# Step sizes of a Mamba block: x products ahead of the dt products, du turned in two halves around them, and ScalarE's copies in that order

## The chip, the cores and the metric

The kernel runs on one core of one Trainium2 chip. The metric is the device time of one execution in microseconds, the median of several executions. Five engines run their own instruction streams and meet only at semaphores: TensorE (PE), VectorE (DVE), ScalarE (ACT), GpSimd (POOL) and SyncE (SP, which here issues the DMAs). Each takes its instructions in the order in which they stand, so a wait holds everything behind it on that engine.

## What is computed

The reference is a two-layer network on x of 4 batches x 512 tokens x 256 features. The change touches one stage of the first layer, the step sizes of a Mamba block. Cut to what matters:

```python
u2 = silu(conv(u) + conv_b)                    # 4 x 512 tokens x 512 channels
dbl = u2 @ W_x                                 # 48 columns: dt_low (16), Bm (16), Cm (16)
dt = softplus(dt_low @ W_dt + b_dt)
A = -exp(A_log)
def step(h, inp):                              # the scan that follows
    dA = exp(dt_t[:, :, None] * A)
    h = dA * h + (dt_t * u_t)[:, :, None] * B_t[:, None, :]
    y = einsum('bdn,bn->bd', h, C_t)
```

softplus(v) is computed as max(v, 0) + ln(1 + exp(-|v|)), with a correction for what 1 + e loses in rounding.

## The kernel before

Channels lie on partitions: a batch is 4 chunks (m) of 128 channels x 512 tokens. The stage walks over the batches in the order `ORDER = (2, 3, 0, 1)`; i counts the places in that order, 0 to 3, and h or r is a half (two chunks of channels, or two tiles of tokens). All orders are written out by hand. For each i:

- TensorE. `x_products(i, bank)` (line 911) is 4 products of u2 with W_x into PSUM bank 4 (in the profile, x8 with 512 columns each). Its two waits are on u2 and on ScalarE's copy of the x product before it, since all but the first share bank 4. `dt_products(i, h)` (line 929) is 2 products into banks 2h and 2h + 1 (x4 in the profile); it waits until VectorE has finished the half of the batch before that used these banks. The B columns are transposed into bank 5 (lines 968 to 976). `turn_du(i, banks)` (line 937) transposes du of a batch in two halves of 8 transposes. Through banks (6, 6) the second half waits for ScalarE's copy of the first; this is done for batch i - 1 after `dt_products(i, 1)`.
- ScalarE. For each half, Abs from PSUM, Exp, Ln (lines 1741 to 1745), which wait for the dt products and for VectorE to have read the last `soft_e` and `soft_l` of that half. Between the halves it copies the next x product (`dbl_out`, line 1671) and the B columns out of PSUM. After the second half `turned_du(i - 1)` (line 1702) copies the two turned halves to `duT`.
- VectorE. For each half four instructions (lines 2095 to 2102), the last of which reads PSUM and writes dt; after both halves du = u2 * dt (line 2106). There is one buffer du, so it waits until TensorE has turned both halves of du of the batch before (`s_duT_mm`, line 2105).
- SyncE. For each i it writes the C rows to DRAM, and for i = 1, 2 it spills u2, dt and duT of batch i - 1 (3 MB) once both turned halves are copied (`s_duT` at 2i). VectorE clears `decay` (line 2111) only when the C rows and both spills have landed. After them come a load of weights and the C rows for the scan.

Ahead of the stage, ScalarE's loop (lines 1688 to 1698) applies silu to the gates z (`gate_z`) and to the convolved u (`silu_out`); the last pass does `gate_z(3, 1)` and then `silu_out` of the last half. A table load follows. Behind the stage, TensorE waits for all of dt, does `d_term(0)` (line 949: zeroing and 32 small matmuls of u2 with a diagonal), turns the last du through banks (6, 4), waits for ScalarE's copies, and feeds the scan. The scan is 64 steps (4 batches x 16 states) of two halves, on all of TensorE, ScalarE, VectorE and GpSimd; the other three stages of the network follow it.

Of the kernel before, what the change touches and what calls it, by code (L numbers as in the profile page):

```python
# [19 lines left out]
ACT = mybir.ActivationFunctionType  # L20
AX = mybir.AxisListType.X

P = 128
B, S, D = 4, 512, 256
# [3 lines left out]
TILES = S // P  # L28
DI, NS, RANK, TAPS = 512, 16, 16, 4
M = DI // P  # L30
# [19 lines left out]
ORDER = (2, 3, 0, 1)  # L50
# [49 lines left out]
def program(nc, t_in, out):  # L100
    ctx = ExitStack()
    with ctx:
# [6 lines left out]
        ps = ctx.enter_context(nc.psum_tensor("ps", [P, 8, 512], F32))  # L109
# [12 lines left out]
        ident, ones, mean = w["ident"], w["ones"], w["mean"]  # L122
# [104 lines left out]
        one = sb("one", [P, 2])  # L227
        at = 0
# [3 lines left out]
        duT = [carve(b * BATCH + 2 * M * S, TILES, DI)[0] for b in range(B)]  # L232
        up, conv_end = carve(3 * BATCH + M * S, M, S + TAPS - 1)
        uc, conv_end = carve(conv_end, M, S)
        at = conv_end + 4
        soft_e, _ = carve(at, 2, 2, S)
        soft_l, soft_end = carve(at + M * S, 2, 2, S)
        lo_xc, at = carve(at, C, S)
        lo_sq, at = carve(at, C, S)
        lo_rstd, at = carve(at, S)  # L240
        s2_xc, at = carve(at, C, S)
        s2_sq, at = carve(at, C, S)
        s2_rstd, at = carve(at, S)
        dbl, dbl_end = carve(at, N)
        xn, at = carve(ARENA - B * C * S, B, C, S)
        assert soft_end <= dbl_end - N and dbl_end <= ARENA - B * C * S
        soft_r, at = carve(ARENA - B * C * S, 2, 2, S)
        du, at = carve(at, M, S)
        bt = view(w["k_aff"], [[TILES * NS, B], [NS, TILES], [1, NS]])
        at = 2 * BATCH  # L250
        decay, at = carve(at, 3, 2, S)
        dub, at = carve(at, 2, TILES, DI)
        c_rows, at = carve(at, 2, G, S)
        state, at = carve(at, SLOTS, M, S)
# [5 lines left out]
        ln_xc, at = carve(head_at + 2 * M * S, C, S)  # L260
        ln_sq, at = carve(at, C, S)
        ln_rstd, at = carve(at, S)
# [30 lines left out]
        s_dbl = sem("dbl_ready")  # L293
        s_bc = sem("bc_written")
        s_dt_mm = sem("dt_products")
        s_soft = sem("softplus_parts")
        s_dt = sem("dt_ready")
        s_z_mm = sem("z_products")
        s_sz = sem("gate_ready")
        s_z_out = sem("gates_spilled")  # L300
        s_bt_mm = sem("b_columns_turned")
        s_bt = sem("b_columns_ready")
        s_du = sem("du_ready")
        s_duT_mm = sem("du_turned")
        s_duT = sem("duT_ready")
# [27 lines left out]
        at = 0  # L333
        cw, at = carve(at, COND_W)
# [8 lines left out]
        pw_w, at = carve(at, PARTS * 2 * D)  # L343
# [453 lines left out]
        def _(pe):  # L797
# [113 lines left out]
            def x_products(i, bank):  # L911
                b = ORDER[i]
                pe.wait_ge(s_u2, (b + 2) * M)
                pe.wait_ge(s_dbl, i + 1)
                for m in range(M):
                    last = pe.matmul(ps[0:48, bank, :], w_x[:, m, :], u2[b][:, m, :],
                                     start=(m == 0), stop=(m == M - 1))
                last.then_inc(s_x_mm, 1)
# [15 lines left out]
                                     start=True, stop=True)  # L934
                last.then_inc(s_dt_mm, 1)

            def turn_du(i, banks):
                pe.wait_ge(s_du, i + 1)
                for r in range(2):
                    if i or r:  # L940
                        pe.wait_ge(s_duT, 2 * i + (r if banks[0] == banks[1] else 0))
                    for t in (2 * r, 2 * r + 1):
                        for m in range(M):
                            last = pe.transpose(ps[:, banks[r] + t % 2, m * P:(m + 1) * P], du[:, m, t * P:(t + 1) * P],
                                                ident)
                    last.then_inc(s_duT_mm, 1)

            nought = one[:, 1:2].bitcast(BF16)[:, 0:1]

# [10 lines left out]

            pe.wait_ge(s_mam, 32)
            pe.wait_ge(s_up, (B + 1) * M)
            for i, b in enumerate(ORDER):
                pe.wait_ge(s_dbl, i + 2)
                dt_products(i, 0)
                if 0 < i < B - 1:
                    x_products(i + 1, 4)
                if i:
                    pe.wait_ge(s_bt, i)
                else:  # L970
                    pe.wait_ge(s_sz, 2 * B)
                for t in range(TILES):
                    last = pe.transpose(ps[:, 5, t * 64:(t + 1) * 64], dbl[0:64, b * S + t * P:b * S + (t + 1) * P],
                                        ident[0:64, 0:64])
                last.then_inc(s_bt_mm, 1)
                dt_products(i, 1)
                if i == 0:
                    x_products(1, 4)
                else:
                    turn_du(i - 1, (6, 6))  # L980
            pe.wait_ge(s_dt, 2 * B)
            d_term(0, range(TILES))
            pe.wait_ge(s_dbl, B + 1)
            pe.wait_ge(s_bt, B)
            turn_du(B - 1, (6, 4))
            pe.wait_ge(s_duT, 2 * B)
            pe.wait_ge(s_ends, 1)

# [566 lines left out]
        def _(act):  # L1555
# [104 lines left out]
            def silu_out(b, chunks):  # L1660
                for m in chunks:
                    act.wait_ge(s_cv, b * M + m + 1)
                    act.activation(u2[b][:, m, :], uc[:, m, :], ACT.Silu,
                                   bias=wm["conv_b"][:, m:m + 1]).then_inc(s_u2, 1)

            def gate_z(i, h):
                act.wait_ge(s_z_mm, 2 * i + h + 1)
                act.activation(z_stage[ORDER[i]][:, 2 * h:2 * h + 2, :], ps[:, 4 + 2 * h:6 + 2 * h, :],
                               ACT.Silu).then_inc(s_sz, 1)

            def dbl_out(i, bank):
                act.wait_ge(s_x_mm, i + 1)
                act.activation(dbl[0:48, tok(ORDER[i])], ps[0:48, bank, :], ACT.Copy).then_inc(s_dbl, 1)
# [14 lines left out]
            for b in range(B):  # L1688
                if ORDER[b] == 0:
                    act.wait_ge(s_xh0, 1)  # L1690
                for h in range(2):
                    gate_z(b, h)
                    silu_out(b, halves[h])
                    if b == B - 1 and h == 0:
                        act.wait_ge(s_rows, 1)
                        dbl_out(0, 0)
                    if b + 1 < B:
                        tap_in(b + 1, halves[h])

            act.preload_act_table_set("natural_log_exp_and_others")  # L1700
            def turned_du(i, banks):
                if ORDER[i] == 0:
                    act.wait_ge(s_z_out, 32)
                for r in range(2):
                    act.wait_ge(s_duT_mm, 2 * i + r + 1)
                    act.activation(duT[ORDER[i]][:, 2 * r:2 * r + 2, :], ps[:, banks[r]:banks[r] + 2, :],
                                   ACT.Copy).then_inc(s_duT, 1)

            def times_b(k):
                b, n = divmod(k, NS)  # L1710
# [22 lines left out]
                act.wait_ge(s_g_turned, b + 1)  # L1733
                act.activation(view(zT[b], [[S, 2], [1, S]]), ps[:, 0:2, :], ACT.Copy).then_inc(s_g01, 1)

            for i, b in enumerate(ORDER):
                for h in range(2):
                    act.wait_ge(s_dt_mm, 2 * i + h + 1)
                    if i:
                        act.wait_ge(s_dt, 2 * i - 1 + h)  # L1740
                    act.activation(soft_e[:, h], ps[:, 2 * h:2 * h + 2, :], ACT.Abs)
                    act.drain()
                    act.activation(soft_e[:, h], soft_e[:, h], ACT.Exp, scale=-1.0)
                    act.drain()
                    act.activation(soft_l[:, h], soft_e[:, h], ACT.Ln, bias=one[:, 0:1]).then_inc(s_soft, 1)
                    if h == 0:
                        if i < B - 1:
                            dbl_out(i + 1, 4)
                        act.wait_ge(s_bt_mm, i + 1)
                        act.activation(bt[:, b], view(ps[:, 5, :], [[64, TILES], [1, NS]], RANK), ACT.Copy).then_inc(s_bt, 1)  # L1750
                if i:
                    turned_du(i - 1, (6, 6))
            act.wait_ge(s_ends, 1)
            act.drain()
            times_b(0)
            turned_du(B - 1, (6, 4))
            act.wait_ge(s_dt, 2 * B)

            for k in range(B * NS):
# [974 lines left out]
```

## Time and profile before

| | us |
|---|---|
| median of 3 runs | 1590.73 (1586.46 to 1591.49) |
| profiled execution, own time | 1589.1 |
| its span, first to last instruction | 1587.3 |
| outside the span | 1.8 |
| TensorE matmul busy | 1444.7 (91%) |
| VectorE busy | 1069.1 (67%) |
| ScalarE busy | 854.5 (54%) |
| mean granted TensorE clock | 0.957 of 2.4 GHz |

Busy shares are means over many stages, so the stage of the change has to be read by itself: it lies at about 253 to 323 us of the span. In the timelines a row is one instruction, or a run of the same instructions; "x4" is their number, and a bracket gives the idle time of the engine just before and who ended it. Times are microseconds from the start of the span.

### The profile page before, as it was taken

The numbers are of one execution on the slowest core, as the hardware profiler recorded it, in microseconds if no ns is written. First come the engines' busy times: TensorE is split into PE (matmuls) and PEld (weight loads), VectorE is DVE, ScalarE is ACT, GpSimd is POOL, SyncE is SP. The second block draws the span as 40 slices with busy tenths as digits, with TensorE's granted clock in tenths as the row PEclk, the third lists the DMA queues.
The fourth block names the chain that finished last, engine by engine and source line by source line (L and its number), as shares of the span: only waits on it lengthen the run. The fifth ranks groups of instructions, "written<-read, shape, count | busy, mean of one in ns | idle before, by whom it ended". The sixth has DMA issues, their size and how long they took to land.

```text
span 1587.3 us, 20216 instructions
## 1 busy us (share of the span) xinstructions
PE 1444.7 (91%) x7408; PEld 985.7 (62%) x7420; DVE 1069.1 (67%) x1219; ACT 854.5 (54%) x1509; POOL 477.4 (30%) x140
## 2 busy tenths in 40 slices
PE   5898798689898999998999899999989999999997
PEld 3576343488797979753443333333358888888886
DVE  6996495789899898864443557777564565565645
ACT  3433455599899898631342267777732433333332
POOL 0999020079788888400321420000000000000000
PEclk7899999799999999978999989999999999999999
DMA  7110010502232211402112122443000000000000
GB/s 269 24 61 1 1 53 2 200 31 91 97 104 107 68 66 41 163 1 41 42 38 72 59 80 61 119 132 123 1 0 0 1 14 1 0 14 1 14 1 14
DMA packets 36624, 87.61 MB, mean 55 GB/s; under 512 B 8350, under 2 KB 24948, under 8 KB 32948
## 3 DMA queue, kind: packets, MB, share of 16 engines
q1 hardware_dynamic: 36532, 86.39, 16.3%
q8 instruction: 57, 0.93, 0.2%
q14 instruction: 35, 0.29, 0.1%
HBM read 68.10 MB, written 18.21 MB: 54 GB/s over the span
## 4 chain that ended last, share of the span: by engine, by line
PE 55%; DVE 2%; ACT 2%; issue 2%; DVEq 1%; ACTq 0%
PE ps L1440 12%; PE ps L1449 12%; PE ps L1308 4%; PE ps L1381 4%; PE ps L1175 3%; PE ps L1296 3%; PE ps L1201 2%; PE ps L1137 2%; PE ps L1008 1%; ACT arena L1909 1%; PE ps L584 1%; PE ps L1350 1%; PE ps L1059 1%; PE ps L1209 1%; PE ps L1187 1%
## 5 line engine op out<-in xcount | busy, mean ns | idle before, releaser
L2593 POOL TENSOR_TENSOR arena<-arena 128x2048 f32<-128x2048 f32 x63 | 287.4, 4591 | 158.4 <-DVE arena L2133 158.3
L2133 DVE TENSOR_TENSOR_SCAN arena<-arena,ps 128x1024 f32<-128x1024 f32 x128 | 284.6, 2272 | 40.2 <-issue 20.7
L1728 ACT ACTIVATE arena<-arena,mam 128x511 f32<-128x511 f32 x256 | 165.8, 710 | 32.0 <-DVE arena L2133 32.0
L1909 ACT ACTIVATE arena<-ps,rho 128x512 f32<-128x512 f32 x256 | 159.1, 689 | 31.4 <-PE ps L1381 30.0
L2365 DVE TENSOR_REDUCE mxs<-ps 128x1 f32<-128x512 f32 x224 | 141.2, 684 | 45.2 <-PE ps L1296 43.3
L996 PE MATMUL ps<-early,arena 128*128 128x128 f32 x768 | 130.1, 278 | 20.3 <-DVE arena L2133 15.0
L1440 PE MATMUL ps<-early,arena 128*128 128x256 f32 x512 | 127.1, 380 | 2.9 <-DVE mam L2532 1.9
L1938 ACT ACTIVATE arena<-arena 128x256 f32<-128x256 f32 x192 | 85.5, 500 | 81.5 <-DVE arena L2536 50.7
L2573 POOL TENSOR_TENSOR arena<-arena 128x4096 f32<-128x4096 f32 x16 | 115.0, 7191 | 43.5 <-DVE arena L2051 43.5
L1716 ACT ACTIVATE arena<-arena,early 128x512 f32<-128x512 f32 x192 | 123.9, 709 | 4.4 <-DVE arena L2111 4.4
L1449 PE MATMUL ps<-arena 128*128 128x256 f32 x512 | 121.0, 379 | 1.2 <-issue 1.2
L1008 PE MATMUL ps<-early,arena 128*128 128x128 f32 x1024 | 121.1, 272 | 0.9 <-POOL arena L2593 0.7
L1008 PEld LDWEIGHTS ps<-early,arena 128*128 128x128 f32 x1024 | 113.8, 140 | 1.2 <-POOL arena L2593 0.8
L996 PEld LDWEIGHTS ps<-early,arena 128*128 128x128 f32 x768 | 90.3, 142 | 35.9 <-DVE arena L2133 21.9
L1440 PEld LDWEIGHTS ps<-early,arena 128*128 128x128 f32 x512 | 96.3, 190 | 19.1 <-DVE mam L2532 3.1
L1449 PEld LDWEIGHTS ps<-arena 128*128 128x128 f32 x512 | 97.2, 190 | 14.8 <-issue 1.5
L1938 ACT ACTIVATE arena<-ps,arena 128x256 f32<-128x256 f32 x64 | 26.9, 471 | 142.6 <-PE ps L1440 142.6
L1381 PE MATMUL ps<-arena 97*128 97x512 bf16 x256 | 97.0, 389 | 6.0 <-ACT arena L1909 4.4
L997 PE MATMUL ps<-arena 128*128 128x128 f32 x512 | 99.4, 276 | 0.0
L1440 PE MATMUL ps<-arena 128*128 128x256 f32 x384 | 98.8, 380 | 0.0
L2532 DVE TENSOR_TENSOR mam<-mam,ps 128x512 f32<-128x512 f32 x32 | 22.0, 687 | 97.0 <-PE ps L1440 97.0
L1296 PE MATMUL ps<-arena 96*128 96x512 bf16 x224 | 86.6, 387 | 0.0
(352 smaller groups left out, 2482.1 us busy)
## 6 DMA issues: line engine op xcount, KB each, us to landing
arena<-bc_scratch SPq DMA_DIRECT2D x32, 512.0 KB, 3.7
arena<-in_ffn SPq DMA_DIRECT2D x8, 1024.0 KB, 5.1
batch_scratch<-arena SPq DMA_DIRECT2D x2, 3072.0 KB, 8.8
arena<-batch_scratch SPq DMA_DIRECT2D x6, 1024.0 KB, 6.9
arena<-q_scratch SPq DMA_DIRECT2D x96, 64.0 KB, 2.2
arena<-k_scratch SPq DMA_DIRECT2D x96, 64.0 KB, 2.2
arena<-in_dec_w SPq DMA_DIRECT2D x1, 3855.0 KB, 16.2
arena<-in_cond SPq DMA_DIRECT2D x1, 3739.5 KB, 11.6
```

The source lines that it names most:

```text
L996: pe.transpose(ps[:, FEED + m, t * P:(t + 1) * P], dub[:, k % 2, t, m * P:(m + 1) * P], ident)
L1008: last = pe.matmul(ps[:, t, m * P:(m + 1) * P], state[:, k % SLOTS, m, t * P:(t + 1) * P], ident, start=False, stop=(k % NS == NS - 1 and ...
L1296: pe.matmul(ps[:, (hg + s) % 3, :], q[0:STACK, i, qc * P:(qc + 1) * P], k[0:STACK, i, :], start=True, stop=True).then_inc(s_s_mm, 1)
L1381: pe.matmul(ps[:, 3 + (hg + n) % 3, :], k[0:STACK + 1, i, kc * P:(kc + 1) * P], q[0:STACK + 1, i, :], start=True, stop=True).then_inc(s_t_ ...
L1440: done = pe.matmul(ps[:, bank, i * S // 2:(i + 1) * S // 2], weights[:, f, :], x, start=first and i == 0, stop=last and i == 1, skip_group ...
L1449: done = pe.matmul(ps[:, bank, half * S // 2:(half + 1) * S // 2], weights[:, f, :], x[:, i, :], start=(r == 0 and half == 0 and i == 0), ...
L1716: act.activation(dub[:, k % 2, t, :], duT[b % 2][:, t, :], ACT.Copy, scale=bt[:, b, t, n:n + 1])
L1728: last = act.activation(decay[:, (2 * k + h) % 3, i, 1:S], dt[b % 2][:, m, 1:S], ACT.Exp, scale=a_neg[:, m * NS + n:m * NS + n + 1])
L1909: act.activation(pt[:, j % 4, i], ps[:, 3 + (hg + n) % 3, :], ACT.Exp, scale=rho[:, 0:1]).then_inc(s_pt, 1)
L2133: dve.tensor_tensor_scan(half, view(decay[:, (2 * k + h) % 3], [[1, 2 * S]]), view(ps[:, FEED + 2 * h, :], [[1, 2 * S]]), 0.0, ALU.mult, A ...
L2365: dve.tensor_reduce(mxs[:, hg % 2, qc, i:i + 1], ps[:, (turn + s) % 3, :], AX, ALU.max).then_inc(s_max, 1)
L2593: pool.tensor_tensor(state[:, k % SLOTS], state[:, k % SLOTS], view(c_rows[:, j % 2, k % G, :], [[0, M], [1, S]]), ALU.mult).then_inc(s_hc, 1)
```

## The change

On TensorE `turn_du` becomes one half (i, r) at a time and the B columns get a function. The loop now issues, for i = 1, 2, 3: the first half of turning du of batch i - 2, the x products of batch i + 1, `dt_products(i, 0)`, the second half of turning du of batch i - 2, the B columns, `dt_products(i, 1)`. Before the loop stands batch 0 with `x_products(1)`, behind it both halves for batch B - 2. Thus the x products of batch i + 1 come before the dt products of batch i, where they came after the first half of them. ScalarE follows in the same order; `dbl_out(i + 2)` now ends the round of batch i, and turned halves 0 and 1 of a batch are copied at the end of one round and in the middle of the next. In the gate loop the last silu of u2 is taken ahead of the last gate. VectorE's, GpSimd's and SyncE's programs are the same. (B = 4.)

```diff
-            def turn_du(i, banks):
+            def turn_du(i, r, bank):
                 pe.wait_ge(s_du, i + 1)
-                for r in range(2):
-                    if i or r:
-                        pe.wait_ge(s_duT, 2 * i + (r if banks[0] == banks[1] else 0))
...
+                if i or r:
+                    pe.wait_ge(s_duT, min(2 * i + r, 2 * B - 2))
...
-            for i, b in enumerate(ORDER):
+            pe.wait_ge(s_dbl, 2)
+            dt_products(0, 0)
+            turn_bc(0)
+            dt_products(0, 1)
+            x_products(1, 4)
+            for i in range(1, B):
+                if i >= 2:
+                    turn_du(i - 2, 0, 6)
+                if i + 1 < B:
+                    x_products(i + 1, 4)
                 pe.wait_ge(s_dbl, i + 2)
                 dt_products(i, 0)
-                if 0 < i < B - 1:
-                    x_products(i + 1, 4)
...
+                if i >= 2:
+                    turn_du(i - 2, 1, 6)
+                turn_bc(i)
                 dt_products(i, 1)
-                if i == 0:
-                    x_products(1, 4)
-                else:
-                    turn_du(i - 1, (6, 6))
+            for r in range(2):
+                turn_du(B - 2, r, 6)
             pe.wait_ge(s_dt, 2 * B)
             d_term(0, range(TILES))
...
-            turn_du(B - 1, (6, 4))
+            for r in range(2):
+                turn_du(B - 1, r, 6 - 2 * r)
...
                 for h in range(2):
-                    gate_z(b, h)
-                    silu_out(b, halves[h])
+                    if b == B - 1 and h == 1:
+                        silu_out(b, halves[h])
+                        gate_z(b, h)
+                    else:
+                        gate_z(b, h)
+                        silu_out(b, halves[h])
...
+            for i in range(B):
+                softplus_parts(i, 0)
+                bt_out(i)
+                if i == 0:
+                    dbl_out(1, 4)
+                if i >= 2:
+                    turned_du(i - 2, 1, 6)
+                softplus_parts(i, 1)
                 if i:
-                    turned_du(i - 1, (6, 6))
+                    turned_du(i - 1, 0, 6)
+                if i + 2 < B:
+                    dbl_out(i + 2, 4)
+            turned_du(B - 2, 1, 6)
             act.wait_ge(s_ends, 1)
             act.drain()
             times_b(0)
-            turned_du(B - 1, (6, 4))
+            for r in range(2):
+                turned_du(B - 1, r, 6 - 2 * r)
```

## Rows read from the trace of the kernel before

**Rows 1.** The page: length of the profiled execution.
```profile
span 1587.3 us, 20216 instructions
```

**Rows 2.** Waits, 253 to 322.6: engine, line, releaser: us in total, times, longest.
```profile
DVE arena L2095 <- ACT arena L1745: 20.3, 6, 12.6
PE ps L944 <- ACT arena L1706: 11.5, 3, 4.6
```

**Rows 3.** Timeline of VectorE in the stage: start, us, instruction, [idle before].
```profile
260.48 0.69 DVE L2095 TENSOR_SCALAR arena<-arena 128x1024 f32<-128x1024 f32 x1 [12.63 <-ACT arena L1745]
...
265.09 0.69 DVE L2095 TENSOR_SCALAR arena<-arena 128x1024 f32<-128x1024 f32 x1
...
269.77 2.29 DVE L2106 TENSOR_TENSOR arena<-arena 128x2048 f32<-128x2048 f32 x1
272.41 0.70 DVE L2095 TENSOR_SCALAR arena<-arena 128x1024 f32<-128x1024 f32 x1 [0.34 <-ACT arena L1745]
...
279.36 0.69 DVE L2095 TENSOR_SCALAR arena<-arena 128x1024 f32<-128x1024 f32 x1 [2.35 <-ACT arena L1745]
...
312.09 2.29 DVE L2106 TENSOR_TENSOR arena<-arena 128x2048 f32<-128x2048 f32 x1
```

**Rows 4.** Timeline of ScalarE in the stage.
```profile
254.44 1.32 ACT L1663 ACTIVATE arena<-arena,mam 128x512 f32<-128x512 f32 x2
...
257.08 1.02 ACT L1741 ACTIVATE arena<-ps 128x1024 f32<-128x1024 f32 x1
...
261.11 0.59 ACT L1673 ACTIVATE arena<-ps 48x512 f32<-48x512 f32 x1 [0.66 <-PE ps L916]
...
261.71 1.01 ACT L1741 ACTIVATE arena<-ps 128x1024 f32<-128x1024 f32 x1
...
279.23 1.00 ACT L1706 ACTIVATE arena<-ps 128x1024 f32<-128x1024 f32 x1
```

**Rows 5.** Timeline of TensorE in the stage, and at one place of the scan.
```profile
257.44 3.63 PE L916 MATMUL ps<-arena,mam 128*48 128x512 f32 x8
265.22 3.75 PE L933 MATMUL ps<-arena,mam 128*128 128x512 f32 x4 [4.15 <-DVE arena L2101]
...
280.29 1.10 PE L944 MATMUL ps<-early,arena 128*128 128x128 f32 x8 [3.49 <-ACT arena L1706]
...
288.64 1.98 PE L933 MATMUL ps<-arena,mam 128*128 128x512 f32 x4
290.46 1.04 PE L944 MATMUL ps<-early,arena 128*128 128x128 f32 x8
294.99 1.97 PE L944 MATMUL ps<-early,arena 128*128 128x128 f32 x8 [3.49 <-ACT arena L1706]
...
325.76 0.91 PE L996 MATMUL ps<-early,arena 128*128 128x128 f32 x3 [2.14 <-ACT arena L1717]
```

**Rows 6.** Stretches: from:to, length, TensorE busy, granted clock, DMA share, GB/s.
```profile
261.00:312.00 51.00, 32.48 (x101) 0.80 0.37 147
265.00:271.00 6.00, 5.78 (x7) 0.50 0.00 0
312.00:315.00 3.00, 2.54 (x11) 0.50 0.39 157
```

**Rows 7.** Timeline of SyncE's queue: second spill, C rows for the scan.
```profile
298.05 0.34 SPq L692 DMA_DIRECT2D batch_scratch<-arena  x1
...
307.40 0.91 SPq L703 DMA_DIRECT2D arena<-bc_scratch  x2
```

**Rows 8.** Timeline of the stage's end: d term, and the first scan instruction.
```profile
312.46 1.91 PE L956 MATMUL ps<-diag,arena 128*128 128x128 f32 x8 [3.29 <-DVE arena L2101]
...
318.13 1.91 PE L944 MATMUL ps<-early,arena 128*128 128x128 f32 x16
...
322.63 2.29 DVE L2133 TENSOR_TENSOR_SCAN arena<-arena,ps 128x1024 f32<-128x1024 f32 x1 [8.05 <-PE ps L997]
```

**Rows 9.** The page, costliest groups: the scan on VectorE.
```profile
L2133 DVE TENSOR_TENSOR_SCAN arena<-arena,ps 128x1024 f32<-128x1024 f32 x128 | 284.6, 2272 | 40.2 <-issue 20.7
```

More of the change, by code:

```diff
@@ L935, in dt_products, with turn_bc @@
                 last.then_inc(s_dt_mm, 1)
-            def turn_du(i, banks):
+            def turn_du(i, r, bank):
                 pe.wait_ge(s_du, i + 1)
-                for r in range(2):
-                    if i or r:
-                        pe.wait_ge(s_duT, 2 * i + (r if banks[0] == banks[1] else 0))
[L942 to L946, printed above, removed]
+                if i or r:
+                    pe.wait_ge(s_duT, min(2 * i + r, 2 * B - 2))
+                for t in (2 * r, 2 * r + 1):
+                    for m in range(M):
+                        last = pe.transpose(ps[:, bank + t % 2, m * P:(m + 1) * P], du[:, m, t * P:(t + 1) * P], ident)
+                last.then_inc(s_duT_mm, 1)
+            def turn_bc(i):
+                if i:
+                    pe.wait_ge(s_bt, i)
+                else:
+                    pe.wait_ge(s_sz, 2 * B)
+                at = ORDER[i] * S
+                for t in range(TILES):
+                    last = pe.transpose(ps[:, 5, t * 64:(t + 1) * 64], dbl[0:64, at + t * P:at + (t + 1) * P],
+                                        ident[0:64, 0:64])
+                last.then_inc(s_bt_mm, 1)
             nought = one[:, 1:2].bitcast(BF16)[:, 0:1]
@@ L962, in _ @@
             pe.wait_ge(s_up, (B + 1) * M)
-            for i, b in enumerate(ORDER):
+            pe.wait_ge(s_dbl, 2)
[8 more added lines that the diff above has]
+                    x_products(i + 1, 4)
                 pe.wait_ge(s_dbl, i + 2)
                 dt_products(i, 0)
-                if 0 < i < B - 1:
-                    x_products(i + 1, 4)
-                if i:
-                    pe.wait_ge(s_bt, i)
-                else:
[L971 to L975, printed above, removed]
+                if i >= 2:
+                    turn_du(i - 2, 1, 6)
+                turn_bc(i)
                 dt_products(i, 1)
-                if i == 0:
-                    x_products(1, 4)
-                else:
-                    turn_du(i - 1, (6, 6))
+            for r in range(2):
+                turn_du(B - 2, r, 6)
             pe.wait_ge(s_dt, 2 * B)
@@ L1691, in _ @@
                 for h in range(2):
-                    gate_z(b, h)
-                    silu_out(b, halves[h])
+                    if b == B - 1 and h == 1:
+                        silu_out(b, halves[h])
+                        gate_z(b, h)
+                    else:
+                        gate_z(b, h)
+                        silu_out(b, halves[h])
                     if b == B - 1 and h == 0:
@@ L1700, in _, with turned_du, bt_out, softplus_parts @@
             act.preload_act_table_set("natural_log_exp_and_others")
-            def turned_du(i, banks):
+            def turned_du(i, r, bank):
                 if ORDER[i] == 0:
                     act.wait_ge(s_z_out, 32)
[L1704 to L1707, printed above, removed]
+                act.wait_ge(s_duT_mm, 2 * i + r + 1)
+                act.activation(duT[ORDER[i]][:, 2 * r:2 * r + 2, :], ps[:, bank:bank + 2, :], ACT.Copy).then_inc(s_duT, 1)
+            def bt_out(i):
+                act.wait_ge(s_bt_mm, i + 1)
+                act.activation(bt[:, ORDER[i]], view(ps[:, 5, :], [[64, TILES], [1, NS]], RANK), ACT.Copy).then_inc(s_bt, 1)
+            def softplus_parts(i, h):
+                act.wait_ge(s_dt_mm, 2 * i + h + 1)
+                if i:
+                    act.wait_ge(s_dt, 2 * i - 1 + h)
+                act.activation(soft_e[:, h], ps[:, 2 * h:2 * h + 2, :], ACT.Abs)
+                act.drain()
+                act.activation(soft_e[:, h], soft_e[:, h], ACT.Exp, scale=-1.0)
+                act.drain()
+                act.activation(soft_l[:, h], soft_e[:, h], ACT.Ln, bias=one[:, 0:1]).then_inc(s_soft, 1)
             def times_b(k):
@@ L1734, in turned_back @@
                 act.activation(view(zT[b], [[S, 2], [1, S]]), ps[:, 0:2, :], ACT.Copy).then_inc(s_g01, 1)
[L1736 to L1750, printed above, removed]
+            for i in range(B):
[6 more added lines that the diff above has]
+                softplus_parts(i, 1)
                 if i:
-                    turned_du(i - 1, (6, 6))
+                    turned_du(i - 1, 0, 6)
+                if i + 2 < B:
+                    dbl_out(i + 2, 4)
+            turned_du(B - 2, 1, 6)
             act.wait_ge(s_ends, 1)
```

## The prediction

> **What bounds the kernel now.** The page gives the length [rows 1], and no share of it helps: this change moves work in 60 us out of 1587. So I asked for the waits of that stretch [rows 2], then for the timelines of its engines. In the waits VectorE stands for ScalarE's Ln, 20.3 us, of which 12.6 is the wait for its first half; the other 7.7 us are five gaps. TensorE stands 11.5 us for ScalarE's copy of a turned half of du, each time with the next dt products behind it in its queue. VectorE's timeline [rows 3] shows the beat: a half takes 4.61 us (260.48 to 265.09), the second half 4.68 up to du, du 2.29 and about 0.05 to the next, 11.6 us a batch. Its five gaps (0.34 and 2.35 stand in the rows) are those 7.7 us. VectorE is the engine with most to do here, and after its last dt all else waits (TensorE's d term [rows 8], ScalarE by way of du and the memset). So the stage is worth at most those gaps, and the question is whether TensorE and ScalarE now stay ahead.
>
> **Why the gaps are there.** Abs to VectorE's start takes 3.40 us (257.08 to 260.48) [rows 3, 4]. dt products at full clock take 1.98 us, x products 3.63, a half turning 1.04; at half clock the first is 3.75 and the last 1.97 [rows 5]. Before, the turning waits inside itself for a copy (3.49 us idle at 280.29), and only behind it do the dt products stand, though their banks were free long ago. That lateness reaches VectorE.
>
> **Part 1, silu ahead of the last gate.** ScalarE waits for the last z products at that place, so the two silus (1.32 us, [rows 4]) fit into that wait, and table load and first Abs come 1.3 us earlier: VectorE's first half starts at 259.2. Its second half gains nothing of it: ScalarE copies x(1) before the second Abs, and x(1) ends at 257.44 + 3.63 = 261.07 [rows 5] as before. With the B columns' copy now ahead of that one, Abs starts at 261.6 instead of 261.71 and VectorE's second half at 265.0. Worth 0.1 us, at least 0 and at most 1.3.
>
> **Part 2, the new order, walked through at full clock.** A wait's release costs about 0.05 to 0.14 us (VectorE's half is over at 265.08, TensorE starts at 265.22 [rows 5]). x(2): 261.75 to 265.4 (needs the copy of x(1), which ends at 261.7). It now lies where TensorE stood idle 4.15 us. Then:
>
> - dt(1,0) 265.3, Abs 267.35, ready for VectorE 270.75; wanted at 272.0 (after du(0)). 1.3 us to spare.
> - dt(1,1) released by VectorE at 269.75; ready 275.2; wanted 276.65.
> - first half of du(0) 272.05 to 273.1, x(3) to 276.7, dt(2,0) released at 276.8; ready 282.2; wanted 283.65 (after du(1)). Second half of du(0) 278.7 to 279.75: its copy of the first half ended at 276.2 on ScalarE (behind the softplus, 275.2). du(1) needs it at 281.3.
> - dt(2,1) 281.4, ready 286.85, wanted 288.3.
> - first half of du(1) to 284.75; dt(3,0) 288.4, ready 293.85, wanted 295.2; second half of du(1) to 291.45, wanted by du(2) at 292.9.
> - dt(3,1) 293.0, ready 298.45, wanted 299.8. du(2)'s halves to 296.35 and 300.5; du(3) wants the last at 304.4.
>
> Everything is 1.3 us or more early, so VectorE runs without a gap from 265.0: du(0) at 269.7, then three batches of 11.6 from 272.0, end 306.85. Before it was 312.09 + 2.29 = 314.38 [rows 3]. Gain 7.5 us. ScalarE has per batch two times 3.4, two copies of du at 1.0, a copy at 0.6 [rows 4] and a small one: under 9.8 of 11.6, and no copy stands long enough before a softplus to use up the 1.3.
>
> **Part 3, the clock.** Here the walk is weakest: at half clock a dt product is 1.77 us longer (3.75 - 1.98) and a turned half 0.93, more than is to spare. In the trace the clock is 0.50 from 265 to 271 [rows 6], after TensorE's idle 4.15 us; one turned half behind an idle 3.49 us ran in 1.97, another behind the same idle in 1.10; and in the scan three transposes took 0.91 after only 2.14 us idle [rows 5]. The new order leaves idle 2.15 us before dt(1,1), 3.6 before dt(3,0), 3.2 before the last half of du(2) and about 3.4 before the d term (3.29 before [rows 8]). dt(1,1) late by 1.77 costs 0.3; dt(3,0) late costs VectorE 0.4, or with the turned half behind it at half clock too 1.77 + 0.93 - 1.45 = 1.25. The bounds are 0 and 1.6 us; as idle of 3.5 was followed by half clock in the rows and the turned half behind it may be at either, I take 0.5. Net 7.0.
>
> The Trainium skill, "TensorE: Matmul & The Clock Gate", section on HAM oscillation in real kernels, says that each burst that follows an idle gap in a loop begins throttled again. By that rule every one of the four gaps is followed by half clock and the gain is nearer 6; by the turned half at 1.10 us it need not be. Half clock itself, 0.50, is in this trace.
>
> **Part 4, the queues and the tail.** The second spill waits for both halves of du(1) copied: 295.0 instead of 298.05. Before, 9.35 us after it SyncE issued the C rows, having seen it landed [rows 7]; so landed by 304.4, and the memset wants it at 306.85. The first spill goes 0.9 us later (283.35) and nobody waits. Should softplus and copy slip 2.5 us, the spill would set the end: the cover is thin. From the last dt to the first scan there are 10.6 us before (312.0 to 322.63 [rows 8]), the same instructions after; with the clock at 0.50 from 312 to 315 [rows 6]. All at full would give 1.5 back, all at half cost about 4.5: TensorE's work in it goes from 312.46 to 318.13 + 1.91 = 320.04 [rows 8], and its last 5 us would double, less what starts beside other work. I take 0, the idle ahead of it being equal.
>
> **The scan and the rest.** 128 scans of 2.27 us with 40 us idle in all [rows 9] and what follows hang on each other by semaphores and start earlier by the same amount; no transfer in it has a fixed time. Kept: 7.0, between 4 and 8.5.
>
> **Sum.** Profiled execution 1589.1 (span 1587.3 and 1.8 around it): 7.0 less is 1582.1. It lies 1.6 under the median of the runs, 1590.73; from the median, **1583.7 us**, 0.44% faster.
>
> **Rivals.**
> - *Clock falls on x(3) too.* x(3) at half is 3.6 us longer, dt(2,0) behind it 1.8: 5.4 less 1.45 to spare is 4 late, with what befalls dt(3,0) some 5; gain 2.5, 1588. For it: TensorE is busy 32 of 51 us with a mean clock of 0.80 [rows 6], and x(3) comes 3.3 us after the 2.15 idle. Against: in those 3.3 us it is nearly always busy, and the new order packs the same work tighter.
> - *Won and given back in the tail.* The 10.6 us from dt to scan run at half clock: 4.5 off, gain 2.5, 1588. For: the idle ahead of the d term. Against: it was the same before, and the clock was back within it.
> - *Slower: TensorE in the stage at half clock from x(2) on.* x 7.2, dt 3.8, a turned half 1.97. Walked as above: dt(1,0) ready at 276.2, dt(2,0) at 293.8 after x(3) to 286.6, du(2) held to 305.1 by its turned half, last du ends about 320, 5.7 later than before, and the tail 3 more: 1599. It decides once both x products in front of dt products are slow; one alone isn't enough (gain 2.5 above). Then the old order was better, with its x products behind. Against: before, 3.49 us of waits came each round, and still half the stage had full clock.
> - *It isn't done.* x products two ahead need bank 4 copied early; dbl_out(3) stands behind softplus(1,1) and a copy of du. The walk says that this binds nobody, but if a copy sits waiting ahead of a softplus the gaps stay: 1590.
>
> **Chances.** Forecast (gain over 4.8) 0.66; clock on x(3) 0.12; tail 0.10; not done 0.05; slower 0.07. A difference of 0.3%, 4.8 us, is about what a measurement can tell from none. The middle ones are "same" but for a share 0.04 that is still faster: faster 0.70, same 0.22, slower 0.08. Range: the best case is 7.6 + 1.5 off the median, 1581.6, and the runs themselves lie up to 4 us below it: 1580; above I include both middle rivals, 1589.5.
>
> **What would show it.** VectorE without gaps from du(0) on, du(3) ending near 307 and the first scan near 315.5; x(2) beginning at 261.8; no wait of `turn_du` for ScalarE over 0.2 us except in the last; spill 2 issued at 295. Wrong if VectorE still waits for Ln between 272 and 304, if the memset waits for a spill, or if the first scan comes 7 us earlier and the end doesn't.

## The result, and the profile after

| | runs | us, median (lowest to highest) | ratio to the kernel before, 95% interval |
|---|---|---|---|
| before, in the first comparison | 6 | 1588.2 (1584.25 to 1591.49) | |
| changed, first comparison | 6 | 1578.79 (1572.96 to 1585.28) | 0.994 (0.9914 to 0.9966) |
| changed, second (a_again) | 12 | 1580.79 (1572.87 to 1584.06) | 0.9966 (0.995 to 0.9982) |
| changed, third (a_third) | 12 | 1582.69 (1578.54 to 1585.84) | 0.9966 (0.9949 to 0.9984) |

The change makes the kernel faster, as forecast: by 0.3 to 0.6%, and none of the three intervals reaches 1. The 1578.79 us lie 4.9 under the forecast 1583.7 and 1.2 under the range. Over all runs of these three comparisons and of the one between them the kernel before has 94 runs with a mean of 1586.5, the changed one 30 with a mean of 1580.9: 5.6 us apart (the two standard errors, 0.33 and 0.61, give it 0.7). The third comparison ran on another chip than the second, with the same ratio. So of the first difference, 9.4 us, some 4 were chance, and of the forecast gain, 7.0, some 1.4 were not kept, which is two standard errors.

Names as in the prediction: x(i) are the x products of batch i, dt(i,h) the dt products of its half h, du(i) its du; i counts from 0, so dt(3,0) is the first half of the last batch.

The profiled execution of the changed kernel took 1585.28 us; it was the slowest of its six. Its page:

```profile
span 1583.5 us, 20233 instructions
PE 1446.7 (91%) x7420; PEld 986.6 (62%) x7420; DVE 1068.9 (67%) x1219; ACT 855.5 (54%) x1509; POOL 477.9 (30%) x140
```

The busy times are those of before. What moved is seen in VectorE's timeline of the stage, which answers to [rows 3] (here the stage began 1.9 us later: its first dt product at 255.19 against 253.32):

```profile
261.13 0.69 DVE L2118 TENSOR_SCALAR arena<-arena 128x1024 f32<-128x1024 f32 x1 [11.41 <-ACT arena L1733]
...
266.85 0.70 DVE L2118 TENSOR_SCALAR arena<-arena 128x1024 f32<-128x1024 f32 x1 [1.12 <-ACT arena L1733]
...
271.54 2.29 DVE L2129 TENSOR_TENSOR arena<-arena 128x2048 f32<-128x2048 f32 x1
...
282.93 2.29 DVE L2129 TENSOR_TENSOR arena<-arena 128x2048 f32<-128x2048 f32 x1
...
295.20 2.29 DVE L2129 TENSOR_TENSOR arena<-arena 128x2048 f32<-128x2048 f32 x1 [0.97 <-PE ps L943]
...
306.58 2.29 DVE L2129 TENSOR_TENSOR arena<-arena 128x2048 f32<-128x2048 f32 x1
```

A line with no bracket followed the instruction ahead of it (often one that is left out here) with no idle time that the profile shows. The five waits for ScalarE's Ln after the first half are down to one of 1.12 us. From one du to the next are 11.39 us. The only new gap, 0.97 us, is du(2) waiting for the turned half of du(1). TensorE's timeline shows why; it answers to [rows 5]:

```profile
263.71 3.60 PE L916 MATMUL ps<-arena,mam 128*48 128x512 f32 x8 [0.77 <-ACT arena L1683]
...
271.50 1.98 PE L933 MATMUL ps<-arena,mam 128*128 128x512 f32 x4 [1.88 <-DVE arena L2124]
273.89 1.09 PE L943 MATMUL ps<-early,arena 128*128 128x128 f32 x8 [0.40 <-DVE arena L2129]
274.92 3.63 PE L916 MATMUL ps<-arena,mam 128*48 128x512 f32 x8
278.48 1.98 PE L933 MATMUL ps<-arena,mam 128*128 128x512 f32 x4
...
289.87 3.75 PE L933 MATMUL ps<-arena,mam 128*128 128x512 f32 x4 [3.50 <-DVE arena L2124]
293.41 1.75 PE L943 MATMUL ps<-early,arena 128*128 128x128 f32 x8
```

x(2) fills the idle time of before, dt products are released by VectorE and no longer by ScalarE's copies, x(3) runs at full clock, and dt(3,0) is at half clock behind 3.50 us of idle, which the turned half behind it shares (1.75 us, against 1.04 at full clock). SyncE's queue, after [rows 7]:

```profile
298.08 0.34 SPq L692 DMA_DIRECT2D batch_scratch<-arena  x1
...
307.42 0.91 SPq L703 DMA_DIRECT2D arena<-bc_scratch  x2
```

The spill is issued at 298.08 and the C rows 9.34 us later, at 307.42, as before; the memset came at 309.01. The cover was 1.6 us here (1.5 to 1.9 in the five profiles), not 2.4. The spill left 1.2 us later here than forecast, counted from the first dt product: the copy that it waits for stands behind the softplus of dt(3,0), which was late with the slow dt product.

To see where the time is won and lost, each profile is cut at five events: first dt product, end of the last du, start of the first scan, start of the last scan, end of the span. Stretches in us, each read from the lines of those instructions (four profiles of the unchanged kernel before, five of the changed one; look_a1 to look_b2 are told of below):

| profile | to the stage | stage | last du to first scan | scan | rest |
|---|---|---|---|---|---|
| before | 253.3 | 61.1 | 8.2 | 330.1 | 934.6 |
| before again (d_null) | 253.4 | 61.2 | 8.3 | 330.1 | 931.1 |
| before, look_b1 | 253.2 | 60.7 | 8.9 | 331.7 | 932.8 |
| before, look_b2 | 254.0 | 60.8 | 9.1 | 331.7 | 933.3 |
| changed | 255.2 | 53.7 | 9.2 | 331.8 | 933.6 |
| changed, a_again | 253.3 | 52.8 | 9.4 | 331.7 | 935.0 |
| changed, a_third | 253.0 | 52.8 | 9.4 | 331.7 | 933.8 |
| changed, look_a1 | 254.9 | 53.5 | 9.1 | 331.6 | 927.6 |
| changed, look_a2 | 253.4 | 52.9 | 9.2 | 331.7 | 933.6 |

By their means the stage gives 7.8 us, the tail (from the last du to the first scan) takes 0.6 back and the scan 0.8: 6.3 won, with the 5.6 of the runs in reach.

Why the tail is longer can be read from the clock. In all nine profiles there is one last stretch at half clock, as long in each, that begins within 2 us of the start of the last turned half of du(2). Here it is in the profile before and in a_again (columns as in [rows 6]):

```profile
305.30:315.40 10.10, 4.91 (x21) 0.50 0.59 198
```

```profile
299.50:309.60 10.10, 7.18 (x32) 0.50 0.82 291
```

What differs is where the d term falls in it. Its first products began 7.2, 7.1, 5.8 and 5.5 us behind the fall of the clock in the four profiles before, and 5.4 to 4.8 us behind it in the five of the changed kernel; the tails, 8.2 to 9.4 us, grow in just that order, by half a us for each us that more of it lies at half clock.

### The profile page after: what moved, and what is told of

Same layout as the page of the kernel before. It is cut to its first block, busy times and chain, and to the rows that moved or that the text cites. A ratio compares the mean times of both kernels' runs of the same rounds, so it can differ in the third digit from the quotient of the medians.

```text
span 1583.5 us, 20233 instructions
## 1 busy us (share of the span) xinstructions
PE 1446.7 (91%) x7420; PEld 986.6 (62%) x7420; DVE 1068.9 (67%) x1219; ACT 855.5 (54%) x1509; POOL 477.9 (30%) x140
## 4 chain that ended last, share of the span: by engine, by line
PE 55%; DVE 2%; ACT 2%; issue 2%; DVEq 1%; ACTq 0%
PE ps L1450 12%; PE ps L1459 12%; PE ps L1318 4%; PE ps L1391 4%; PE ps L1185 3%; PE ps L1306 3%; PE ps L1211 2%; PE ps L1147 2%; PE ps L1018 1%; ACT arena L1932 1%; PE ps L584 1%; PE ps L1360 1%; PE ps L1069 1%; PE ps L1219 1%; PE ps L1197 1%
## 5 line engine op out<-in xcount | busy, mean ns | idle before, releaser
L1006 PEld LDWEIGHTS ps<-early,arena 128*128 128x128 f32 x768 | 89.6, 142 | 36.6 <-DVE arena L2156 20.3
## 6 DMA issues: line engine op xcount, KB each, us to landing
arena<-in_cond SPq DMA_DIRECT2D x1, 3739.5 KB, 11.6
```

The costliest lines, as they stand in the source:

```text
L1006: pe.transpose(ps[:, FEED + m, t * P:(t + 1) * P], dub[:, k % 2, t, m * P:(m + 1) * P], ident)
```

## Experiments

**The same two kernels again.** d_null is the kernel before against itself, a_again and a_third are the changed one.

> The kernel before against itself. Theory: ratio 1 within 0.2%, with single runs spread over 5 to 7 us, and a profile whose stage takes 60 to 62 us again while the first 250 us and the 930 us behind the scan move by 1 to 3 us with the clock. Rival: the stage itself varies by several us from run to run, so one profile doesn't measure it.

> The changed kernel once more, unchanged. Theory: the change is worth the five gaps of VectorE in the stage, 7 to 7.5 us, and nothing elsewhere; the 9.4 us between the medians hold some 2 us of chance. Then this run lies 6 to 8.5 us under the kernel before (ratio 0.9947 to 0.9962), and in its profile the stage (first dt product to end of the last du) again takes 53 to 54.5 us against 61.1. Rival: there is a second gain behind the stage, and the difference is again 9 us or more with segments behind the first scan shorter by 2 us.

> The changed kernel for the third time, beside the last one. Theory: 6.3 us (0.4%) under the kernel before, as over the runs so far; single times from 1573 to 1585 with the mean granted clock, low clock high time. Rival: the 5.4 us of the second series or the 9.4 us of the first are the true value, 0.34% or 0.6%.

d_null: 1.0001 (0.9987 to 1.0015); 12 runs from 1582.42 to 1590.98, a wider spread than the 5 to 7 us expected, and the part behind the scan moved by 3.5 us, not 1 to 3. a_again and a_third: 0.9966 twice, 4.8 and 5.3 us between the medians. The stage repeats within 1 us. So a_again missed the 6 to 8.5 us of its theory, since the tail and the scan give some back; the first difference was too large by chance, and the rival of a second gain behind the stage has nothing to show. a_third's own theory of 6.3 us was a little high, and the rival's 5.4 nearer.

**The parts of the change.** c_order is the changed kernel with `gate_z` ahead of the last `silu_out`; b_silu has that swap alone:

```diff
 b_silu: the kernel before
-                    gate_z(b, h)
-                    silu_out(b, halves[h])
+                    if b == B - 1 and h == 1:
+                        silu_out(b, halves[h])
+                        gate_z(b, h)
+                    else:
+                        gate_z(b, h)
+                        silu_out(b, halves[h])
```

> The changed kernel with the gate ahead of the last silu, as before: the new order alone. Theory: VectorE's first half starts 1.3 us later, but its second half doesn't, since ScalarE's copy of x(1) sets that; so the end of the last du moves by 0 to 0.1 us and the gain is the whole 7 us. Rival: the silu place is worth 1.3 us of it.

> The kernel before with only the last silu ahead of the last gate. Theory: VectorE starts 1.3 us earlier and loses it before its second half; dt(1,0) is released 1.3 us earlier, but VectorE then waits for dt(1,1) and the turning as before: 0 to 0.5 us gained in all, the same as before within what is measured. Rival: 1.3 us gained.

c_order: 0.9971 (0.9952 to 0.999), stage 52.8 us, last du to first scan 9.4, the same as with the swap. As far as the stage shows, the whole gain is the new order's. b_silu: 0.9996 (0.9982 to 1.0009). Its stage took 59.6 us against 60.7 to 61.2 in the four profiles before, so it was 1.1 to 1.7 shorter, more than expected: VectorE waited 0.34 us in batch 1, where it waited 1.5 to 2.8 before. The tail was 9.1. A gain of 1.3 us isn't excluded by the interval, which reaches to 2.8.

**Turning as before, x ahead (e_x_ahead); x behind, turning moved (f_turn_split).**

```diff
 e_x_ahead: the changed kernel
-                if i >= 2:
-                    turn_du(i - 2, 0, 6)
...
-                if i >= 2:
-                    turn_du(i - 2, 1, 6)
                 turn_bc(i)
                 dt_products(i, 1)
+                for r in range(2):
+                    turn_du(i - 1, r, 6)
 f_turn_split: the changed kernel
-                if i + 1 < B:
-                    x_products(i + 1, 4)
                 pe.wait_ge(s_dbl, i + 2)
                 dt_products(i, 0)
+                if i + 1 < B:
+                    x_products(i + 1, 4)
```

(ScalarE's copies are moved with them: in e both turned halves behind softplus(i,1) and ahead of `dbl_out(i + 2)`, in f `dbl_out(i + 1)` behind softplus(i,0).)

> The changed kernel with du turned as before: both halves of du(i-1) behind dt(i,1), on TensorE and on ScalarE. Theory (the wait for ScalarE's copy inside the turning is what delays the dt products): the turning again holds the queue, x(3) starts only behind its second half (278.9 on the scale of the first profile of the changed kernel, there 274.9), dt(2,0) reaches VectorE 2.5 to 3 us late, later ones up to 1 us: the stage takes 56 to 57.5 us, against 53 to 54 changed and 61.2 before. Rival (the place of the x products is the whole gain): the stage stays at 53 to 54.

> The changed kernel with the x products behind dt(i,0) again, and their copies between the halves, so only the turning is moved. Theory: dt(2,0) is on time, but x(3) now stands ahead of the second half of du(0), which du(1) waits for, 2.1 us late; behind it all is late by that: stage 55 to 56 us. Rival (the turning is the whole gain): 53 to 54. Other rival (x behind dt costs a round's 3.6 us each time): 58 or more.

Both stages came out longer than their theories: 58.7 and 58.2 us. In e VectorE waits 4.34 us for dt(2,0), in f 5.11 us for the turned half that du(1) needs. The 58.2 is in the range of f's other rival (58 or more), but not by its mechanism: the x products cost VectorE this one long wait, not 3.6 us in each round. TensorE in the one and in the other:

```profile
277.30 1.87 PE L943 MATMUL ps<-early,arena 128*128 128x128 f32 x8 [2.96 <-ACT arena L1715]
279.11 4.46 PE L916 MATMUL ps<-arena,mam 128*48 128x512 f32 x8
283.50 1.98 PE L933 MATMUL ps<-arena,mam 128*128 128x512 f32 x4
```

```profile
278.33 3.75 PE L933 MATMUL ps<-arena,mam 128*128 128x512 f32 x4 [3.50 <-DVE arena L2122]
282.01 4.72 PE L916 MATMUL ps<-arena,mam 128*48 128x512 f32 x8
286.67 1.10 PE L943 MATMUL ps<-early,arena 128*128 128x128 f32 x8
```

The walk at full clock had the right mechanism in each (turning behind a copy; x products ahead of the turning), and was short by the half clock that follows the idle time: in e 0.83 + 0.83 us on the turned half and x(3), in f 1.77 + 1.09 on dt(2,0) and x(3). In the changed order x(3) stands in what was idle, and runs in 3.63 us. By time: e 0.9948 (0.9929 to 0.9968), f 0.9997 (0.9978 to 1.0015). f's stage gained 2.9 us, and its interval reaches to 3.5. e doesn't agree with its stage: 2.4 us of stage against 8 us of time. It has 6 runs; its profiled one, 1585.86, was the slowest, and the other five lie at 1579.6 to 1581.1 with a mean clock of 0.965 to 0.966, against 0.961. Which stretch those five saved isn't known. So by the times alone e is as fast as the changed kernel (a mean of 1581.1 against 1580.9), and they don't exclude the rival that the place of the x products is the whole gain. That the turning has its share rests on the one profile of e: 58.7 us of stage, where five profiles of the changed kernel show 52.8 to 53.7.

**Doubled x(3) (h_x3_twice).**

```diff
+                for again in range(2 if i == B - 1 else 1):
                     for m in range(M):
                         last = pe.matmul(ps[0:48, bank, :], w_x[:, m, :], u2[b][:, m, :],
```

> The changed kernel with the x products of the last batch done twice, 3.6 us more on TensorE ahead of dt(2,0). This prices the rival in which the clock is at half on x(3). Theory: dt(2,0) has 1.4 us to spare, so VectorE gets it 2.2 us late: stage 55 to 56 us, 2 us of the gain lost. Rival (TensorE's queue sets the stage now): the whole 3.6 us are lost, 56.5 to 57.5. Other rival: nothing lost.

Stage 56.0 us, 0.9978 (0.9962 to 0.9994). VectorE waits 1.97 us for the turned half of du(0), then 0.23 for dt(2,0): 2.2 of the 3.6 us, as worked out, so the slack was 1.4. At du(2) it waits 1.14 more, for a turned half at half clock (1.92 us), as the changed kernel did in two of its five profiles (0.97 and 0.85).

**One VectorE instruction less in either kernel (i_less_before, i_less_after).** The output then lacks part of the rounding correction.

```diff
-                    dve.tensor_tensor(soft_r[:, h], soft_e[:, h], soft_r[:, h], ALU.subtract)
-                    dve.drain()
```

> The kernel before with one of VectorE's four instructions per half left out (the subtraction of the rounding correction, 1.30 us with its start, 8 times: 10.4 us less on VectorE; dt then lacks the right correction). Theory: before the change a loop of TensorE and ScalarE alone sets the beat (second half of turning, dt(i,0), x, dt(i,1), softplus, copy of the first half, second half of turning: 14.7 us from 280.29 to 294.99), VectorE isn't in it, so only its last batch gets shorter: stage 57.5 to 59 us against 61.2, 2 to 4 us gained. Rival: VectorE bounded before too, and 8 to 10 us are gained.

> The changed kernel with the same instruction left out. Theory: after the change VectorE sets the beat (11.4 us a batch), so its 10.4 us come off until ScalarE, 9.5 us a batch, or the way from VectorE's end over dt and softplus (5.5 us) is next: stage 44 to 47 us against 52.8 to 53.7, 7 to 9 us gained. Rival: TensorE or ScalarE bound already after the change, and 2 to 4 us are gained as in the kernel before.

With 10.4 us less on VectorE, the kernel before shortened its stage by 5.2 us (61.1 to 55.9), the changed one by 6.6 (52.8 to 46.2); times 0.9976 (0.9956 to 0.9996) and 0.992 (0.9891 to 0.9949). The changed one's stage is within its 44 to 47 us, its saving just under the 7 to 9. The first is more than the 2 to 4 expected: VectorE's last batch gives 2.6 by itself, and the waits of VectorE for ScalarE went from 20.3 us [rows 2] to 25.5, so half of the saving turned into waits. In that kernel TensorE and ScalarE keep their beat, from one second turned half to the next:

```profile
277.65 1.41 PE L944 MATMUL ps<-early,arena 128*128 128x128 f32 x8 [3.49 <-ACT arena L1706]
292.38 1.97 PE L944 MATMUL ps<-early,arena 128*128 128x128 f32 x8 [3.48 <-ACT arena L1706]
304.36 1.97 PE L944 MATMUL ps<-early,arena 128*128 128x128 f32 x8 [4.55 <-ACT arena L1706]
```

277.65 to 292.38 is 14.73 us; with the whole of VectorE's work it was 14.70 (280.29 to 294.99 [rows 5]). The next interval, in which no x products stand, is 11.98 against 12.21. So this loop set the middle of the stage before, and VectorE did not. After the change VectorE's saving shows until the next things come up, and one of them is the DMA of which the prediction had said that its cover is thin; the memset now waits for it:

```profile
301.73 0.06 DVE L2132 MEMSET arena<- 128x6 f32 x1 [1.88 <-DMA bc_scratch<-arena]
```

**TensorE kept busy in its idle places (g_busy, g_again).** The matmuls are of zeros, into a bank that is free.

```diff
+            def busy(n):
+                for _ in range(n):
+                    pe.matmul(ps[:, 4, :], nought.to_broadcast([P, P]), nought.to_broadcast([P, S]), start=True, stop=True)
...
+                if i == B - 1:
+                    busy(12)
                 dt_products(i, 0)
...
-            for r in range(2):
-                turn_du(B - 2, r, 6)
+            turn_du(B - 2, 0, 6)
+            busy(12)
+            turn_du(B - 2, 1, 6)
+            busy(8)
             pe.wait_ge(s_dt, 2 * B)
             d_term(0, range(TILES))
```

> The changed kernel with matmuls of zeros (bf16, 128 x 512, into bank 4) in three idle places of TensorE: 12 before dt(3,0), 12 between the last two halves of du(2), 8 before the d term. Theory (the clock halves because TensorE idles there): the granted clock stays at 1.00 from 285 to 313, VectorE's 1 us before du(2) goes, and last du to first scan falls from 9.3 to 6.8 us, so 3 to 3.5 us are gained on the changed kernel. Rival (these idle times don't set the clock, or zeros don't hold it): both stay, and the time is the same or 0.5 us longer.

> The changed kernel with 32 zero matmuls in TensorE's idle places once more, beside the changed kernel. Theory: the d term at full clock is worth 2.8 us, so it lies 2 to 4 us under the changed kernel and 8 to 11 under the one before; stage 52.8 and last du to first scan 6.6 us again. Rival: its 9.9 us were chance, and it equals the changed kernel within 1 us.

Stage 52.8 and last du to first scan 6.6 us, both times. Granted clock, in a_again during its d term and in g_busy over its last 28 us up to the scan (columns as in [rows 6]):

```profile
304.00:309.00 5.00, 4.79 (x21) 0.50 0.76 218
```

```profile
285.00:313.00 28.00, 21.94 (x131) 1.00 0.69 271
```

and in g_busy the start of the d term, whose first eight products with the diagonal took 1.91 us before [rows 8]:

```profile
304.26 0.39 PE L967 MATMUL ps<-one 128*128 128x512 bf16 x1 [2.13 <-DVE arena L2132]
304.49 1.05 PE L969 MATMUL ps<-diag,arena 128*128 128x128 f32 x8
```

So with the idle time filled the clock stays up, and matmuls of zeros are enough to fill it. Ratios 0.9924 (0.99 to 0.9948) and 0.9937 (0.9915 to 0.9958). Over both, 18 runs have a mean of 1576.6 us (standard error 0.93): 4.3 under the changed kernel, 9.9 under the one before. This version beats both. Its tail is 2.7 us shorter and its stage 0.3 than the means of the changed kernel's profiles; the other 1.3 is about one standard error.

**Where the spread lies (look_a1, look_a2, look_b1, look_b2).** The unchanged kernels, a profile each.

> The changed kernel, one look. Theory (the spread is the clock's course outside the stage): stage 52.8 to 53.7 and last du to first scan 9.2 to 9.5 us again, and the span's difference from 1582 lies in the first 253 us, the scan and the stages behind it. Rival: the stage or its tail moves by 2 us or more.

> The changed kernel, a second look, with the same question. Theory: stage 52.8 to 53.7, last du to first scan 9.2 to 9.5 us, the scan 330 to 331.8, the rest 929 to 935. Rival: the stage or its tail moves by 2 us or more.

> The kernel before, one look. Theory: stage 61.1 to 61.3, last du to first scan 8.2 to 8.3, scan 330.1 again; what differs from 1587.3 lies before the stage and behind the scan. Rival: the stage differs by 1 us or more, and the gain in it with it.

> The kernel before, a second look, with the same question. Theory: stage 61.1 to 61.3, last du to first scan 8.2 to 8.3, scan 330.1. Rival: the stage differs by 1 us or more.

Times 1578.6, 1582.57, 1589.13 and 1590.65. In the table above stage and tail move by at most 0.9 us within a kernel, while the part before the stage moves by 2.2 and the rest by 7.4. For the kernel before the theory was too strict: tail and scan aren't fixed at 8.2 and 330.1 but were 8.9 and 9.1, and 331.7, in these two profiles, and the stage was 60.7 and 60.8. In the scan the 1.6 us are one wait of VectorE of 4.85 us, in look_b1 at 435 and in look_b2 at 522, where in the other batches it is 3.2:

```profile
435.44 4.46 DVE L2133 TENSOR_TENSOR_SCAN arena<-arena,ps 128x1024 f32<-128x1024 f32 x2 [4.85 <-issue]
520.85 4.46 DVE L2133 TENSOR_TENSOR_SCAN arena<-arena,ps 128x1024 f32<-128x1024 f32 x2 [3.21 <-issue]
```

```profile
434.83 4.46 DVE L2133 TENSOR_TENSOR_SCAN arena<-arena,ps 128x1024 f32<-128x1024 f32 x2 [3.19 <-issue]
521.91 4.46 DVE L2133 TENSOR_TENSOR_SCAN arena<-arena,ps 128x1024 f32<-128x1024 f32 x2 [4.85 <-issue]
```

In a_again the clock is below full at that place, 0.72 over the six us in which TensorE, idle 2.1 us just before, works off the d term and the state sum:

```profile
421.00:427.00 6.00, 5.57 (x35) 0.72 0.01 3
```

This slow place came in all five profiles of the changed kernel and in two of the four before. The variants go either way: c, e and g (both runs) have it, while b, f, h and both of i had a scan of 330.0 to 330.2 us without it, though h and i_less_after have the new order. In the rest, 850 to 950 us has a granted clock of 0.90 in a_again (rest 935.0) and 0.97 in look_a1 (rest 927.6):

```profile
850.00:950.00 100.00, 85.62 (x295) 0.90 0.25 77
```

```profile
850.00:950.00 100.00, 85.60 (x315) 0.97 0.27 81
```

By these means TensorE spent 14 us more of the 100 at half clock in a_again, in which its work takes 7 us longer. That would be nearly all of the 7.4, but it wasn't followed step by step. The mean clock of a run goes with its time: over 88 runs of the kernel before the correlation is -0.80 (at 0.959 and below a mean of 1589.5, at 0.966 of 1583.2), over the 30 of the changed one -0.86.

## Why the prediction was right and wrong

- **Bound of the stage: right in place.** VectorE's gaps were what could be had. In the trace before, the copy inside the turning stands ahead of the late dt products; e and f, the two halves of the change, shorten the stage by 2.4 and 2.9 us in their profiles, and together by 7.8, so it takes both; the times of e don't bear this out, and that stays open. One reading of the waits was off: of the three turned halves that waited for a copy, two had dt products behind them, the last had the d term. i_less_before adds what the prediction only implied: a loop of TensorE and ScalarE set the beat before.
- **Part 1: right.** VectorE starts earlier and waits 1.12 us ahead of its second half, for x(1); c_order shows nothing lost without it.
- **Part 2: right in mechanism, the beat mis-sized.** The slack of 1.4 us held (h_x3_twice), and counted from the first dt product x(2) began within 0.1 us of the forecast 261.8. A batch takes 11.39 us on VectorE, not 11.6: halves back to back start 4.50 us apart, where the 4.61 of [rows 3] had a short wait for ScalarE's Ln in it, and the next half starts 2.21 us after du, not 2.34. Over three batches this is 0.7. So the stage gain at full clock was 8.3 (61.1 to 52.8), not 7.5.
- **Part 3: right.** dt(3,0) is partly or wholly at half clock in each of the five profiles (2.58 to 3.75 us), and du(2) waits between 0 and 0.97 us for the turned half behind it; 0.5 was taken. The rule that the prediction takes from the Trainium skill, "TensorE: Matmul & The Clock Gate", section HAM oscillation, fits dt(3,0) behind 3.50 us of idle, the last half of du(2) behind 3.10 (1.85 to 1.94 us) and the d term, but not dt(1,1), which ran in 1.98 us behind 1.88 us of idle. The Trainium skill tells it of waits that are long enough to bring the clock down; the prediction left this condition out when it applied the rule to all four gaps.
- **Part 4: wrong in the tail and the scan.** "I take 0, the idle ahead of it being equal" failed. The idle ahead of the d term wasn't equal (2.2 to 3.0 us, against 3.3), and it isn't what decides: with 3.3 us of it in all four profiles before, their tails differ by 0.8. What counts is how soon behind the fall of the clock the d term comes, and in the changed kernel it comes sooner. The tail is 0.6 longer in the mean (9.1 to 9.4 us, against 8.2 to 9.1), and the scan, with its slow place, 0.8. These 1.4 us take the stage's 7.8 down to 6.3; that the runs show 5.6 is within one standard error of that. Whether the shift of the stage brings on the scan's slow place, or five profiles are few, stays open.
- **The rivals.** Clock on x(3): didn't happen in this order (x(2) and x(3) took 3.60 to 3.63 us in all five profiles), happened in part in e and f. The tail at half clock all through: not seen. In a_again, the worst, the clock is at half for the first 3.5 of the 9.4 us, and that costs 1.1 against the tail of [rows 8], not 4.5. The slower case and the one in which nothing is done: not seen.
- **Sum: the failing step.** "It lies 1.6 under the median of the runs, 1590.73; from the median, 1583.7" took a median of three as the scale. The kernel before has a mean of 1586.5 over 94 runs, and only 8 of them are at 1590.73 or above. From 1586.5 the same gain gives 1579.5. The low end, 1580, had the best gain off the same high median, and from the 1581.6 that this gave it went down by only 1.6 us, though the prediction itself says that runs lie up to 4 below; the 94 runs span 12 us. The miss of 4.9 us adds up so: 4.2 for the base, plus 2.1 by which the first six runs of the changed kernel lie under the mean of its 30, which is chance, less the 1.4 of the gain that were not kept. So the size of the gain was about right, the base was wrong, and chance put the time outside the range: 1580.9 would have been within it.
- **Signs named ahead.** No wait for Ln between 272 and 304, and no wait of the memset for a spill, as forecast. du(3) ends at 307.0 counted from the first dt product (forecast: near 307), the first scan comes at 316.2 (315.5), and TensorE waits 0.73 us for ScalarE's copy at the first half of du(2), where no more than 0.2 was said.

## What to carry to other kernels

A wait for another engine's copy in the middle of a queue delays all that stands behind it, however early it could have run. Take such two-part work apart and put other work that is ready between the parts, with the slack of each piece written down. Work put into idle time of TensorE can pay twice, since in this kernel half clock followed the longer idle times: x(3) took 3.63 us in the new order, 4.46 and 4.72 in e and f, where it came soon behind idle time. When the gain that is forecast is as small as the spread of single runs, forecast the ratio from the profile, and give the absolute time the width of the base's own runs.

## What the runs showed of the hardware

Zero matmuls (bf16, 128 x 512, twelve in 2.79 us) in three idle places kept the granted clock at 1.00 from 285 to 313 us in g_busy and in g_again, where without them it was at 0.50 from 299.5 to 309.6 in a_again. The first eight products of the d term took 1.05 us instead of 1.91. Behind an idle time of 3.50 us the same dt product, dt(3,0), took 2.62, 2.88 and 3.75 us in three executions of one program (a_again, look_a2, the first profile), so how much of a burst is slow differs from run to run. In the first profile the clock fell during the idle time, at 288.0, and the product began at 289.87; in a_again it fell at 289.2, after the product had begun at 288.01.
